# Attention inside a four-layer kernel: the value products of a step are joined and moved behind the far bias of the step's second piece

## The chip, the cores and the metric

The kernel runs on one core of a Trainium2 chip. The metric is the device time of one execution in microseconds (us). TensorE is called PE in the profile, VectorE is DVE, ScalarE is ACT, GpSimd is POOL, and SyncE (SP) issues the DMAs.

## The reference

Four layers run one after the other; the change touches only the first, an attention with a relative position bias, for 2 batches of 2048 tokens, 16 heads of 16 columns:

```
qkv = x @ W_w.T + W_b                                  # q, k, v: 16 heads of 16
attn = einsum('bhqd,bhkd->bhqk', q, k) / sqrt(256)     # causal: keys after the query are -inf
attn = attn + rpb[key - query + s - 1]                 # one bias per head and distance, clamped at the table's end
w = softmax(attn, axis=-1)
o = einsum('bhqk,bhkd->bhqd', w, v)                    # then projection, residual, layer norms
```

The other three layers (a mixture of cumulative products, a state-space scan, a mixture of 20 experts) follow it and are not changed.

## The kernel before

Each head `p` of the attention takes 10 steps of 4 slots (`STEPS`, `SLOTS`), and each slot works on both batches (`b` is 0 or 1). Two jobs share the slots. For head `p` the *scores* are made with keys on the partitions: a piece is a pair (J, c) of a tile of 128 keys and a chunk of 512 queries, of which only the causal part, 128 to 512 columns, is computed. `SCORED` says which piece stands in which slot. For head `p + 1` the *search* makes the same products with queries on the partitions, so that DVE can find each query's maximum in time for the next head; `SEARCHED` is its order. Its widths in slots 0 to 3 match those that `SCORED` has in the same slots.

On PE one slot is: `score` for b = 0 (L541) beside `search` for b = 1 (L515), then `score` for b = 1 beside `search` for b = 0. The two of a pair use different halves of the array's rows and run side by side; below this is "a pair". Then comes `add_near` (L527), the bias of the searched piece, four matmuls, where that piece has one, and then `add_far` (L557), the bias of the scored piece, twelve matmuls on quarters of the array, where the piece has queries at least 8 tiles after the keys. Only pieces (0, 2), (0, 3), (1, 2), (1, 3), (2, 2), (2, 3), (3, 2), (3, 3), (4, 3), (5, 3), (6, 3) and (7, 3) have such a far bias: two in each of steps 2 to 5, one in each of steps 6 to 9, none in steps 0 and 1.

The *sums* (L584) multiply the probabilities of the step before by the values. A step has two rounds of them. A round is four products, which go to four different groups of 32 columns of the array and run side by side; each product of f32 data is two matmul instructions (a half each). `sums(p, step - 1, turn)` for turn 0 stands between the two pairs of slot 1, and for turn 1 between the two pairs of slot 3.

The results lie in PSUM in two rings of three banks (`RING = 3`). ACT takes the exponential of each score (`exponential`, L644) into `prob`, which is why `score` waits for the exponential of three scores earlier. DVE reduces each searched piece to its row maximum (`largest`, L733; L736 with the causal mask where the piece lies on the diagonal), which is why `search` waits for the reduction of three searches earlier. Turns of the maxima (`turn_max`, L593) and of the outputs (`turn_out`, L600) take their turn in the search's ring. Every engine works strictly in the order of its loop; a wait on PE holds back everything that stands behind it on PE. POOL clears the part above the diagonal (`cut`, L432). `prob` has two buffers, one for each of two neighbouring steps. SP issues the loads of the next heads; the change moves none of them.

Of the kernel before, what the change touches and what calls it, by code (L numbers as in the profile page):

```python
# [66 lines left out]
def after(eng, sem, value):  # L67

    if not isinstance(value, int) or value > 0:
        eng.wait_ge(sem, value)  # L70
# [35 lines left out]
def phase_qkv(nc, t):  # L106
# [14 lines left out]
PAIRS = H  # L121
# [6 lines left out]


SCORED = [[(8, 2), (9, 2), (8, 3), (9, 3)], [(11, 2), (10, 2), (10, 3), (11, 3)],  # L130
# [4 lines left out]
assert [sorted(pieces) for pieces in SCORED] == [[(J, c) for J in keys for c in range(J // TPC, S // CH)] for keys in GROUPS_OF_KEYS]  # L135
SEARCHED = [(15, 0), (14, 3), (15, 1), (15, 2),
# [10 lines left out]
STEPS, SLOTS = len(SCORED), 4  # L147
# [57 lines left out]
def phase_attention(nc, t):  # L205
# [3 lines left out]
    with nc.cleanup_on_exit(), ExitStack() as ctx:  # L209
# [55 lines left out]
        def half(b, rows=P // 2):  # L265
            return slice(b * P // 2, b * P // 2 + rows)
# [203 lines left out]
        def _(eng):  # L470
# [61 lines left out]
            def score(p, step, x, b):  # L532

                J, c = SCORED[step][x]
                lo, hi = max(J * P, c * CH), (c + 1) * CH
                has_far = (J + FAR) * P < hi
                turn = NP2 * p + 2 * (SLOTS * step + x) + b
                after(eng, s2_read, turn - RING + 1)
                if turn == 0:
                    eng.wait_ge(s1_read, ALONE)  # L540
                mm = nc.tensor.matmul(s2[:, turn % RING, 0:hi - lo], ks[p % 3][half(b, ROWS), J * P:(J + 1) * P],  # L541
                                      qs[p % 3][half(b, ROWS), lo:hi], start=True, stop=not has_far)
                if not has_far:
                    mm.then_inc(s2_ready, 1)

            def add_far(p, step, x):

                J, c = SCORED[step][x]
                lo, hi = max(J * P, c * CH), (c + 1) * CH
                far_lo = max(lo, (J + FAR) * P)  # L550
                turn = NP2 * p + 2 * (SLOTS * step + x)
                for part in range(3 if far_lo < hi else 0):
                    for b in range(2):
                        for s in range(2):
                            at = far_lo - (J + FAR) * P + s * P // 2
                            rows = half(1 - s)
                            mm = nc.tensor.matmul(s2[rows, (turn + b) % RING, far_lo - lo:hi - lo], flip_b[half(b), s, rows],  # L557
                                                  far[p % 2][half(b), part, at:at + hi - far_lo], start=False, stop=part == 2)
                        if part == 2:
                            mm.then_inc(s2_ready, 1)  # L560

            def sums(p, step, turn):

                if turn == 0:
                    eng.wait_ge(s2_read, NP2 * p + 2 * SLOTS * (step + 1))
                    eng.wait_ge(cut_done, CUTS[STEPS] * p + CUTS[step + 1])
                if step == 0 and turn == 0:
                    eng.wait_ge(vst_ready, 2 * p + 2)
                    for b in range(2):
                        after(eng, oT_ready[b], p)  # L570
                keys = GROUPS_OF_KEYS[step]
                for b in range(2):
                    for x, (J, c) in enumerate(SCORED[step]):
                        if len(keys) == 1:
                            first = b == 0
                        elif keys[1] - keys[0] == 1:
                            first = J == keys[0]
                        else:
                            first = (J == keys[0]) == (b == 0)
                        if first != (turn == 0):  # L580
                            continue
                        g = c if b == 0 else 3 - c
                        lo = max(J * P - c * CH, 0)
                        mm = nc.tensor.matmul(o_ps[32 * g:32 * g + 32, b, lo:CH], vst[p % 2][b][:, J, :],  # L584
                                              prob[:, b, step % 2, x * CH + lo:(x + 1) * CH],
                                              start=J == (8 if c >= 2 else 0), stop=J == (3, 7, 7, 15 if b == 0 else 7)[c])
                mm.then_inc(summed, 1)
# [15 lines left out]
            for p in range(-1, PAIRS + 1):  # L603
                if p + 1 < PAIRS:
                    eng.wait_ge(stack_ready, 2 * p + 4)
                    eng.wait_ge(near_loaded[(p + 1) % 2], 32 * ((p + 1) // 2 + 1))
                for step in range(STEPS):
                    if 0 <= p < PAIRS and step in (0, 2):
                        eng.wait_ge(row_ready, 4 * p + 2 + step)
                        eng.wait_ge(far_loaded[p % 2], 96 * (p // 2 + 1))  # L610
                    for x in range(SLOTS):
                        for b in range(2):
                            if 0 <= p < PAIRS:
                                score(p, step, x, b)
                            if p + 1 < PAIRS:
                                search(p + 1, SLOTS * step + x, 1 - b)
                            if b == 0 and x in (1, 3) and p >= 0:
                                if step > 0 and p < PAIRS:
                                    sums(p, step - 1, x // 2)
                                if step == 0 and p > 0:  # L620
                                    sums(p - 1, STEPS - 1, x // 2)
                        if p + 1 < PAIRS:
                            add_near(p + 1, SLOTS * step + x)
                        if p == -1 and x % 2 == 1:
                            project(len(USES) - 20 + (SLOTS * step + x) // 2)
                        if 0 <= p < PAIRS:
                            add_far(p, step, x)
                        if (step, x) == (0, 2) and 0 <= p < PAIRS:
                            turn_max(p, 0)
                        if (step, x) == (7, 2) and p + 1 < PAIRS:  # L630
                            turn_max(p + 1, 1)
                        if step == 1 and x in (1, 3) and p > 0:
                            turn_out(p - 1, x // 2)
# [2131 lines left out]
```

## Time and profile before

| | us |
|---|---|
| median of 3 runs | 2643.36 (2638.0 to 2645.14) |
| the profiled execution: span from first to last instruction | 2646.7 (no other time of it is listed) |
| attention, its 16 heads of scores | about 121 to 1085 of the span |
| one head | 60.5 |
| PE busy, whole span | 2472.2 (93%) |
| DVE busy, whole span | 1964.7 (74%) |
| ACT busy, whole span | 1382.1 (52%) |

PE's busy time counts each matmul from its start until its result has landed, so that overlapping matmuls and the tail of the last one are in it; the distance from one start to the next is the better measure of what a piece of PE work costs. A row of the timeline with a count merges neighbouring instructions of one kind; its time runs from the start of the first to the end of the last.

### The profile page before, as it was taken

The page shows a single profiled execution, that of the slowest core. Times are in us where ns is not written, and L with a number is a line of the kernel's source. Part 1 is how long each engine was busy: PE and PEld are TensorE (multiplying, and loading weights), DVE is VectorE, ACT ScalarE, POOL GpSimd, SP SyncE. Part 2 cuts the span into 40 slices and gives each one's busy share as a digit, 9 for nine tenths or more (in the row PEclk, how much of TensorE's full clock was granted, in tenths as well). Part 3 has the DMA queues.
Part 4 walks back from the last instruction along what each step waited for, and adds up shares of the span by engine and source line. Part 5 has one row for each costly group of instructions (what it writes and reads, how often), then busy time and mean ns, then how long its engine had stood idle before and what let it go on. Part 6 is the DMA issues. An engine that isn't in the chain of part 4 may idle for free. (4 is left out here: it accounts for less than half of the span.)

```text
span 2646.7 us, 43896 instructions
## 1 busy us (share of the span) xinstructions
PE 2472.2 (93%) x15059; PEld 1552.6 (59%) x15059; DVE 1964.7 (74%) x4037; ACT 1382.1 (52%) x2469; POOL 1110.7 (42%) x1092
## 2 busy tenths in 40 slices
PE   7999999999999999899999997999999999977992
PEld 4433333333333333467777775888888888855772
DVE  3777777777777774266676657999999999975256
ACT  3466666666666666444455535655555555543320
POOL 3522222222222221110000004999989898944454
PEclk9999999999999999999999998999999999987996
DMA  8633333323333321100000000000000000024785
GB/s 244 174 70 71 82 58 58 58 58 58 58 58 69 70 64 66 54 16 17 16 24 25 9 17 8 13 12 12 12 12 12 12 12 12 4 86 130 238 282 162
DMA packets 109601, 166.41 MB, mean 63 GB/s; under 512 B 15876, under 2 KB 74296, under 8 KB 106232
## 3 DMA queue, kind: packets, MB, share of 16 engines
q1 hardware_dynamic: 99064, 143.24, 21.5%
q0 software_dynamic: 6144, 16.79, 2.0%
q10 hardware_dynamic: 4224, 4.19, 0.5%
q8 instruction: 99, 1.62, 0.3%
q14 instruction: 70, 0.57, 0.1%
HBM read 97.66 MB, written 62.01 MB: 60 GB/s over the span
## 5 line engine op out<-in xcount | busy, mean ns | idle before, releaser
L644 ACT ACTIVATE ssm_in_dt<-att_s 128x512 f32<-128x512 f32 (+3 forms) x1280 | 610.0, 535 | 346.9 <-PE att_s L541 182.7
L733 DVE TENSOR_REDUCE att_partmax<-att_s 128x1 f32<-128x512 f32 x768 | 494.3, 686 | 109.8 <-PE att_s L515 66.4
L541 PE MATMUL att_s<-att_qs,att_ks 49*128 49x512 f32 (+3 forms) x1280 | 433.9, 419 | 16.1 <-ACT ssm_in_dt L644 13.8
L515 PE MATMUL att_s<-att_ks,att_qs 49*128 49x512 f32 (+3 forms) x1280 | 434.5, 424 | 4.9 <-DVE att_qs L723 4.7
L541 PEld LDWEIGHTS att_s<-att_qs,att_ks 49*128 49x128 f32 x1280 | 207.4, 185 | 380.3 <-ACT ssm_in_dt L644 307.6
L1797 POOL TENSOR_TENSOR ssm_cc<-ssm_cc,ssm_h 128x512 f32<-128x512 f32 x256 | 334.9, 1308 | 75.7 <-DVE ssm_h L1858 73.8
L432 POOL TENSOR_SCALAR_AFFINE_SELECT ssm_in_dt<-ssm_in_dt 128x256 f32<-128x256 f32 x256 | 104.6, 409 | 621.5 <-ACT ssm_in_dt L644 562.8
L584 PE MATMUL att_o_ps<-ssm_in_dt,att_vst 128*32 128x512 f32 (+3 forms) x2560 | 340.6, 542 | 5.3 <-ACT ssm_in_dt L644 5.3
L1812 POOL TENSOR_TENSOR ssm_out_z<-ssm_out_z,ssm_cc 128x512 f32<-128x512 f32 x256 | 340.4, 1330 | 0.1
L1737 ACT ACTIVATE ssm_cc<-ssm_c_ps,ssm_cur 128x512 f32<-128x512 f32 x256 | 199.0, 777 | 211.8 <-PE ssm_c_ps L1686 211.5
L736 DVE CUSTOM_DVE_ANT_0 att_hid<-att_s,att_hidden 128x512 bf16<-128x512 f32 (+3 forms) x512 | 238.8, 487 | 94.6 <-PE att_s L515 93.7
L1858 DVE TENSOR_TENSOR_SCAN ssm_h<-ssm_a_ps,ssm_h,ssm_inp 128x512 f32<-128x512 f32 x192 | 243.8, 1270 | 0.1
L1730 ACT ACTIVATE ssm_a_ps<-ssm_in_dt,ssm_cur 128x512 f32<-128x512 f32 x256 | 176.4, 689 | 114.5 <-DVE ssm_h L1858 108.5
L515 PEld LDWEIGHTS att_s<-att_ks,att_qs 49*128 49x128 f32 x1280 | 203.9, 185 | 28.1 <-DVE att_partmax L733 10.8
L1842 DVE SCALAR_TENSOR_TENSOR ssm_inp<-ssm_b_ps,ssm_cur,ssm_in_u 128x512 f32<-128x512 f32 x256 | 190.0, 742 | 34.5 <-PE ssm_b_ps L1686 32.7
L1684 PE MATMUL ssm_b_ps<-ssm_hi,ssm_w_hi 128*128 128x512 f32 x512 | 203.5, 398 | 12.7 <-DVE ssm_lo L1835 11.2
L1684 PE MATMUL ssm_c_ps<-ssm_hi,ssm_w_hi 128*128 128x512 f32 x512 | 203.2, 397 | 0.0
L1685 PE MATMUL ssm_c_ps<-ssm_lo,ssm_w_hi 128*128 128x512 f32 x512 | 203.2, 397 | 0.0
L1686 PE MATMUL ssm_c_ps<-ssm_hi,ssm_w_lo 128*128 128x512 f32 x512 | 202.9, 396 | 0.0
L1686 PE MATMUL ssm_b_ps<-ssm_hi,ssm_w_lo 128*128 128x512 f32 x512 | 202.8, 396 | 0.0
L1685 PE MATMUL ssm_b_ps<-ssm_lo,ssm_w_hi 128*128 128x512 f32 x512 | 202.4, 395 | 0.0
L1850 DVE SCALAR_TENSOR_TENSOR ssm_inp<-ssm_a_ps,ssm_inp 128x512 f32<-128x512 f32 x256 | 169.2, 661 | 0.0
(324 smaller groups left out, 4183.7 us busy)
## 6 DMA issues: line engine op xcount, KB each, us to landing
qk_halves<-ssm_in_dt SPq DMA_DIRECT2D x64, 256.0 KB
moe_sorted<-att_hidden SPq DMA_DIRECT2D x31, 512.0 KB, 9.4
moe_rows<-moe_sorted SPq DMA_DIRECT2D x62, 256.0 KB
moe_answers<-moe_mixed SPq DMA_DIRECT2D x62, 256.0 KB
att_far<-bias_tables SPq DMA_DIRECT2D x96, 136.0 KB, 8.5
att_stage_q<-qk_halves SPq DMA_DIRECT2D x96, 128.0 KB, 4.4
att_stage_k<-qk_halves SPq DMA_DIRECT2D x96, 128.0 KB, 5.9
ssm_raw<-in_w_bc SPq DMA_DIRECT2D x30, 256.0 KB, 2.6
```

What stands on the lines that cost most here:

```text
L515: mm = nc.tensor.matmul(s1[:, S1_BANK[at], 0:hi - lo], qs[p % 3][half(b, ROWS), I * P:(I + 1) * P], ks[p % 3][half(b, ROWS), lo:hi], start ...
L541: mm = nc.tensor.matmul(s2[:, turn % RING, 0:hi - lo], ks[p % 3][half(b, ROWS), J * P:(J + 1) * P], qs[p % 3][half(b, ROWS), lo:hi], start ...
L584: mm = nc.tensor.matmul(o_ps[32 * g:32 * g + 32, b, lo:CH], vst[p % 2][b][:, J, :], prob[:, b, step % 2, x * CH + lo:(x + 1) * CH], start= ...
L644: nc.scalar.activation(prob[:, b, step % 2, x * CH + lo:(x + 1) * CH], s2[:, turn % RING, 0:CH - lo], ACT.Exp, scale=1.0 / HD).then_inc(s2 ...
L733: nc.vector.tensor_reduce(most, piece, AX, ALU.max).then_inc(s1_read, 1)
L736: nc.vector.tensor_tensor_reduce(out=hid[HID[at]][:, 0:width], in0=piece, in1=hidden[:, CH - width:CH], scale=1.0, scalar=-3.0e38, op0=ALU ...
L1684: nc.tensor.matmul(out, w_hi, hi[:, k, tok], start=first, stop=False)
L1685: nc.tensor.matmul(out, w_hi, lo[:, k, tok], start=False, stop=False)
L1686: return nc.tensor.matmul(out, w_lo, hi[:, k, tok], start=False, stop=last)
L1797: nc.gpsimd.tensor_tensor(at, at, h[:, i % H_RING], ALU.mult).then_inc(multiplied, 1)
L1812: nc.gpsimd.tensor_tensor(part, part, cc[:, i % Y_RING], ALU.add).then_inc(y_added, 1)
L1858: nc.vector.tensor_tensor_scan(h[:, i % H_RING], a_ps[:, i % A_RING], inp[:, i % 2], 0.0 if first else h[:, (i - 1) % H_RING, CH - 1:CH], ...
```

## The change

The far pieces of steps 2 to 9 change places with their neighbours, so that slot 1 always holds one of them. Both rounds of sums now stand together, once per step, behind the far bias of slot 1 (in steps 0 and 1, which have no far bias, behind slot 1's pairs and near bias). `SEARCHED` stays as it was.

```diff
 SCORED = [[(8, 2), (9, 2), (8, 3), (9, 3)], [(11, 2), (10, 2), (10, 3), (11, 3)],
-          [(0, 2), (0, 0), (0, 3), (0, 1)], [(1, 2), (1, 0), (1, 3), (1, 1)],
-          [(2, 2), (2, 0), (2, 3), (2, 1)], [(3, 2), (3, 0), (3, 3), (3, 1)],
-          [(4, 3), (4, 1), (12, 3), (4, 2)], [(5, 3), (5, 1), (13, 3), (5, 2)],
-          [(6, 3), (6, 1), (14, 3), (6, 2)], [(7, 3), (7, 1), (15, 3), (7, 2)]]
+          [(0, 0), (0, 2), (0, 3), (0, 1)], [(1, 0), (1, 2), (1, 3), (1, 1)],
+          [(2, 0), (2, 2), (2, 3), (2, 1)], [(3, 0), (3, 2), (3, 3), (3, 1)],
+          [(4, 1), (4, 3), (12, 3), (4, 2)], [(5, 1), (5, 3), (13, 3), (5, 2)],
+          [(6, 1), (6, 3), (14, 3), (6, 2)], [(7, 1), (7, 3), (15, 3), (7, 2)]]
...
                                 score(p, step, x, b)
                             if p + 1 < PAIRS:
                                 search(p + 1, SLOTS * step + x, 1 - b)
-                            if b == 0 and x in (1, 3) and p >= 0:
-                                if step > 0 and p < PAIRS:
-                                    sums(p, step - 1, x // 2)
-                                if step == 0 and p > 0:
-                                    sums(p - 1, STEPS - 1, x // 2)
                         if p + 1 < PAIRS:
                             add_near(p + 1, SLOTS * step + x)
                         if p == -1 and x % 2 == 1:
                             project(len(USES) - 20 + (SLOTS * step + x) // 2)
                         if 0 <= p < PAIRS:
                             add_far(p, step, x)
+                        if x == 1 and p >= 0:
+                            for turn in range(2):
+                                if step > 0 and p < PAIRS:
+                                    sums(p, step - 1, turn)
+                                if step == 0 and p > 0:
+                                    sums(p - 1, STEPS - 1, turn)
```

## Rows read from the trace of the kernel before

**Rows 1.** Stretches: heads 1 to 14, and the last head; busy us by engine.

```profile
core 0: us, PE busy (x) PEld busy (x) DVE busy (x) ACT busy (x) POOL busy (x), PEclk, DMA share, GB/s
182.00:1030.00 848.00, 825.75 (x7310) 330.44 (x7310) 667.41 (x1736) 538.94 (x1134) 209.76 (x334) 1.00 0.32 61
1030.00:1076.00 46.00, 43.83 (x346) 15.04 (x344) 3.45 (x12) 33.47 (x69) 6.97 (x14) 1.00 0.26 95
```

**Rows 2.** Groups by line in 182 to 1030: busy us, mean ns, idle before.

```profile
L515 PE MATMUL att_s<-att_ks,att_qs 49*128 49x512 f32 (+3 forms) x1121 | 387.8, 419 | 0.0
L541 PE MATMUL att_s<-att_qs,att_ks 49*128 49x512 f32 (+3 forms) x1121 | 382.0, 416 | 11.8 <-ACT ssm_in_dt L644 9.9
L584 PE MATMUL att_o_ps<-ssm_in_dt,att_vst 128*32 128x512 f32 (+3 forms) x2240 | 298.0, 540 | 4.3 <-ACT ssm_in_dt L644 4.3
...
L733 DVE TENSOR_REDUCE att_partmax<-att_s 128x1 f32<-128x512 f32 x672 | 433.2, 686 | 89.8 <-PE att_s L515 60.7 <-PE att_s L527 27.1
...
L644 ACT ACTIVATE ssm_in_dt<-att_s 128x512 f32<-128x512 f32 (+3 forms) x1120 | 533.9, 535 | 309.1 <-PE att_s L541 162.0 <-PE att_s L557 146.6
```

**Rows 3.** Timeline of one step: start us, length us, engine, line, count.

```profile
520.85 0.84 PE L557 MATMUL att_s<-att_far,att_flip_b 64*64 64x512 bf16 x12
521.62 0.50 PE L541 MATMUL att_s<-att_qs,att_ks 49*128 49x512 f32 x1
521.73 1.57 ACT L644 ACTIVATE ssm_in_dt<-att_s 128x512 f32<-128x512 f32 x3 [1.35 <-PE att_s L557]
522.05 1.06 PE L584 MATMUL att_o_ps<-ssm_in_dt,att_vst 128*32 128x512 f32 x8
523.05 0.49 PE L541 MATMUL att_s<-att_qs,att_ks 49*128 49x512 f32 x1
523.39 0.61 PE L541 MATMUL att_s<-att_qs,att_ks 49*128 49x512 f32 x2
523.58 0.60 ACT L644 ACTIVATE ssm_in_dt<-att_s 128x512 f32<-128x512 f32 x1 [0.28 <-PE att_s L541]
523.61 0.69 DVE L733 TENSOR_REDUCE att_partmax<-att_s 128x1 f32<-128x512 f32 x1 [0.73 <-PE att_s L515]
523.62 0.39 PE L515 MATMUL att_s<-att_ks,att_qs 49*128 49x512 f32 x1
523.84 0.62 PE L527 MATMUL att_s<-att_near,att_flip_b 64*128 64x512 bf16 x4
```

**Rows 4.** The same timeline, a window later.

```profile
524.07 0.39 PE L527 MATMUL att_s<-att_near,att_flip_b 64*128 64x512 bf16 x2
524.39 0.84 PE L557 MATMUL att_s<-att_far,att_flip_b 64*64 64x512 bf16 x12
524.48 1.29 DVE L733 TENSOR_REDUCE att_partmax<-att_s 128x1 f32<-128x512 f32 x2 [0.17 <-PE att_s L527]
525.16 0.50 PE L541 MATMUL att_s<-att_qs,att_ks 49*128 49x512 f32 x1
...
525.33 0.60 ACT L644 ACTIVATE ssm_in_dt<-att_s 128x512 f32<-128x512 f32 x1 [1.15 <-PE att_s L557]
525.59 0.64 PE L584 MATMUL att_o_ps<-ssm_in_dt,att_vst 128*32 128x512 f32 x4
```

**Rows 5.** Timeline where a search waits for DVE, and a turn of outputs (L600).

```profile
549.13 1.29 DVE L733 TENSOR_REDUCE att_partmax<-att_s 128x1 f32<-128x512 f32 x2 [0.32 <-PE att_s L527]
...
549.88 0.18 PEld L515 LDWEIGHTS att_s<-att_ks,att_qs 49*128 49x128 f32 x1 [0.29 <-DVE att_partmax L733]
...
554.61 0.66 PE L600 MATMUL att_s<-att_ident,att_oT 128*128 128x128 f32 x4
...
555.20 0.49 PE L541 MATMUL att_s<-att_qs,att_ks 49*128 49x512 f32 x1
```

**Rows 6.** The turn of the maxima (L593), same place in two neighbouring heads.

```profile
533.50 0.27 PE L593 MATMUL att_s<-att_ident,att_mx 128*16 128x128 f32 x1 [0.43 <-DVE att_partmax L736]
...
594.05 0.27 PE L593 MATMUL att_s<-att_ident,att_mx 128*16 128x128 f32 x1 [0.43 <-DVE att_partmax L736]
```

**Rows 7.** Timeline after the last score: two rounds of sums back to back.

```profile
1084.06 1.28 PE L584 MATMUL att_o_ps<-ssm_in_dt,att_vst 128*32 128x512 f32 x16 [0.69 <-ACT ssm_in_dt L644]
```

## The prediction

> **What bounds the kernel now.** I read first the busy time of the stretch that the change touches. In heads 1 to 14 PE is busy 825.75 of 848 us, DVE 667.41 and ACT 538.94, with PE's clock at 1.00, the 2.4 GHz level [rows 1]. The groups by line come next: PE's idle time before its matmuls is 11.8 us before L541, 4.3 before L584 and 0.0 before L515 [rows 2], while DVE waited 89.8 us before its reductions and ACT 309.1 us before its exponentials, both for PE. So PE sets the pace, and it hardly waits. One head takes 594.05 - 533.50 = 60.55 us [rows 6], about 16 times.
>
> The third view is the timeline, for starts [rows 3]. A pair that follows work of another shape (far bias or sums) is followed by its neighbour 0.34 us later (523.05 to 523.39); the next pair of the same shape comes 0.23 us after that (523.39 to 523.62). A far bias of 512 columns takes 0.77 (520.85 to 521.62). From the pair at 521.62 to the sums is 0.43, and one round of sums holds PE for 1.00 (522.05 to 523.05). So each change of shape costs about 0.1 us on either side of the sums.
>
> The reader should also see what the sums do for the others. While PE is in a round, DVE and ACT empty their rings of three banks: from 521.73 ACT does three exponentials in 1.57 us, one every (1.57 - 0.60) / 2 = 0.48 us [rows 3], and DVE does two reductions in 1.29 us, one every 0.61 us [rows 4]. Eight searches of 512 columns are 4.9 us of DVE in a step of some 6 us, and two rounds, one in each half of the step, give it that time without PE waiting. That is why PE shows no wait although only three banks stand between.
>
> **What the change removes on PE.** Before, each round costs its 1.00 plus 0.10 to enter and 0.10 in the next pair: 2.40 us for two. Behind a far bias the joined rounds cost only their own length over what "far bias, pair" costs already. That length: the first half of a round lasts 0.64 and the whole 1.06, so a further half adds 0.42 to 0.43 [rows 3, 4]; joined is 1.00 + 2 x 0.43 = 1.86. Saved: 0.54 us in steps 2 to 9. In steps 0 and 1, with no far bias, 0.33. Where widths differ more is saved: 16 matmuls of the last step (products of 512 and 128 columns, each group of columns having one of either) took 1.28 against 1.06 for 8 [rows 7], so the groups run on by themselves, and the joined rounds of the steps with 384, 256 and 128 take some 1.65, 1.43 and 1.24: 0.2 + 0.4 + 0.6 = 1.2 us per head.
>
> On the other side, scores of 512 columns now run beside searches of 384, 256 or 128 in slot 1, and the reverse in slot 0 (steps 3 to 5 and 7 to 9). A pair lasts as long as its wider part; with the halves alternating this costs the difference once, some 0.05, 0.11 and 0.16 us, twice each: 0.6 us. On PE alone the sum per head is 8 x 0.54 + 2 x 0.33 + 1.2 - 0.6 = 5.6 us less, if PE then waits no more than now. The number of far biases, near biases, exponentials, reductions, cuts and DMAs is the same. The cuts come as early or earlier, and the sums ask for them later; `prob` is freed in time (the sums of step s - 2 stand before step s); the copies of the outputs become ready sooner. These are worth nothing, as POOL and SP are idle for most of this stretch (POOL 209.76 of 848 us [rows 1]).
>
> **What it adds: waits in the two rings.** Now PE is away for 1.86 us once, in which DVE can do at most the three searches in its banks, and from there to the next sums come six pairs in a row (slots 2, 3, 0) and two more in slot 1 with nothing between but biases. I work out the time from one joined block to the next, from sums of step 2 to those in step 3, with zero at the start of the block. Used are: pairs 0.34 and 0.23 apart; near bias 0.23 to its second set; that set to DVE 0.41 (524.07 to 524.48 [rows 4]); last far set to ACT 0.42 (its merged row of 0.84 less one matmul of 0.38 puts the last set 0.46 in; 520.85 + 0.46 to 521.73 [rows 3]); reduction 0.69, one per 0.61; from its end to the waiting search 0.06 (549.13 + 0.69 to 549.88 [rows 5]), together 0.74 from a reduction's start.
> - 0 to 1.86: sums. DVE and ACT end by 0.5 and 1.2, then stand idle.
> - Slot 2: pairs at 1.86 and 2.19, near bias 2.42 and 2.65, so DVE starts the first reduction at 3.06 and the second at 3.67. Far bias 2.95 to 3.73; ACT's first exponential at 3.83, the second at 4.31.
> - Slot 3: pair at 3.73; the second pair must wait for that first exponential (3.83 + 0.65 = 4.48). Its reductions start at 4.3 and 5.05.
> - Slot 0: pairs at 4.96 and 5.44, each held by an exponential. The near bias follows, last set at 5.73; DVE starts at 6.14.
> - Slot 1: the second search takes the bank of slot 0's first search, so it waits until 6.14 + 0.74 = 6.88. Then 0.17 of its own, 0.09 to change shape and 0.61 of far bias (384 columns): the next sums start at 7.76.
>
> The trace of before has 6.63 between these places. The same reckoning done for the old order, from the sums of slot 3 in step 2 to those in step 3, gives 6.46; the trace has 6.51, so the method is good to about 1%.
>
> The other steps, worked the same way: DVE's restart, the start of slot 0's first reduction, plus 0.74 (0.35 where it is 128 wide), plus pair and far bias; new time against old:
> - step 3 to 4: 3.06, 6.20, tail 0.66: 7.60 against 6.43
> - 4 to 5 (no near bias in slot 2): 2.42, 5.76, 0.44: 6.94 against 5.72
> - 5 to 6: 2.98, 6.20, 1.09: 8.03 against 6.67
> - 6 to 7: 3.01, then four reductions 5.44, 0.87: 7.05 against 5.75
> - 7 to 8: 2.42, 4.82, 0.66: 6.22 against 5.75
> - 8 to 9: 2.19, 4.12, 0.44: 5.30 against 4.86
> - 9 to 0: 1.99, 4.03, 0.28: 5.05 against 4.71
> - 0 to 1: 2.45, 5.68 (a copy of DVE in between), 0.21: 6.24 against 6.24
> - 1 to 2: the two turns of outputs, 0.59 each (554.61 to 555.20 [rows 5]), delay both ends: 3.65, 6.99, 1.09: 8.82 against 7.80
>
> The differences are 1.13 + 1.17 + 1.22 + 1.36 + 1.30 + 0.47 + 0.44 + 0.34 + 0.00 + 1.02 = 8.45 us per head, 69.0 against 60.6. The 5.6 us saved on PE are in it: the new waits are some 14 us per head. Heads 0 to 14 have a search: 15 x 8.45 = 127 us. In the last head DVE has nothing to reduce (3.45 us busy [rows 1]) and only ACT's ring holds; the same walk gives +0.8 to +1.3 in four steps, a little less than nothing in three, together +4. Sum +131 us: span 2646.7 to 2777, and from the median of the runs, which is 3 us lower, 2643.4 + 131 = 2774.
>
> The unknown prices are the joined length, which lies between 1.43 (the second round costs only its two later halves at half price) and 2.00 (twice the single round), and the reckoning's own 1%, which is 0.7 us a head. As DVE is idle through the block's end, 0.1 us more or less in it is 1 us a head and 15 us in all: -0.3 gives 2730, +0.14 and the loss of the 1.2 us for unequal widths gives 2815. I take 1.86, from the nearest rows [rows 3, 4].
>
> The Trainium skill speaks on both sides. TensorEngine Tiling (Array Packing), section Key Properties, says that a change of the tiling mode drains the engine; the 0.1 us on each side of the sums agree, and by that rule alone the change gains. The same page, PSUM Bottleneck, says that tiling speeds up TensorE but not the emptying of PSUM, which can become the limit; by that rule it loses. The sum above stands on the rows without either.
>
> **Rivals.**
> 1. *Fewer changes of shape are all that counts* (faster). If the rings never held PE: 5.6 x 16 = 90 us less, 2554. For it: PE busy 97% and hardly a wait [rows 1, 2]. Against: that state exists because the sums are spread; eight pairs at 0.23 to 0.34 apart outrun a DVE that needs 0.61 for each.
> 2. *Only ACT's ring holds* (about even). If DVE caught up better than I reckon, exponentials at 0.48 would set the pace: steps 2 to 5 still lose 0.5 to 0.7 each, since slot 2's far bias delays the first exponential to 3.83; the other six gain 3 us together. That is -0.6 us a head, 2634. Against: DVE's reductions are longer than the exponentials, and the wait behind the near bias of slot 0 is one of DVE.
> 3. *The joined rounds don't overlap at all* (slower still): 2815, as above. Against: rows 7.
>
> That the change doesn't do what it says is excluded by the order of the loop.
>
> **How the numbers follow.** Forecast 0.83; rival 3 0.05; rival 2 0.07, about half of it within the bound; rival 1 0.05. A measurement of this kernel tells 0.3%, 8 us, from no change. Slower 0.88, same 0.04, faster 0.08. The likeliest case alone gives 2735 to 2815; the range is 2705 to 2822, on account of a DVE that I have made a little too slow, or two banks that come free sooner.
>
> **What would show it.** The turn of the maxima (L593) should come 69 us after that of the head before. The sums should appear as 16 in one row of about 1.9 us. PE's idle time before L515 should go from 0.0 to several us per head, released by DVE, L541's by ACT; DVE should be idle for 1 to 2 us around each block of sums. PE busy in attention should fall below 90%. I am wrong if the head is near 61 us or less: then the banks were not the limit. I am wrong in the size if the search of slot 1 doesn't wait for the reduction of slot 0.

## The result, and the profile after

The change makes the kernel slower: 2909.16 us, the median of 4 runs (2904.08 to 2913.04), against 2644.01 us for the kernel before in 4 runs (2638.0 to 2645.14). The ratio is 1.0997 (95% interval 1.0974 to 1.102). That is 265 us where I had forecast 131. The sign was right, and so was the mechanism that was forecast, waits at the two rings; but it accounts for half of the loss. The other half comes from something that the forecast did not contain.

The head of the page of the changed kernel, and three stretches of it: heads 1 to 14 without the end, 50 us inside head 0, and most of the last head. Columns as in rows 1; the last but two is PE's granted clock.

```profile
span 2911.3 us, 43896 instructions
...
PE 2706.7 (93%) x15059; PEld 1674.4 (58%) x15059; DVE 1950.5 (67%) x4037; ACT 1364.2 (47%) x2469; POOL 1109.3 (38%) x1092
...
PEclk9999889989889899877999999899999999997997
```

```profile
core 0: us, PE busy (x) PEld busy (x) DVE busy (x) ACT busy (x) POOL busy (x), PEclk, DMA share, GB/s
182.00:1000.00 818.00, 778.41 (x5509) 330.79 (x5505) 494.43 (x1316) 395.08 (x857) 164.38 (x257) 0.89 0.27 52
132.00:182.00 50.00, 47.63 (x385) 19.90 (x389) 32.72 (x75) 26.23 (x54) 9.20 (x16) 1.00 0.33 64
1275.00:1350.00 75.00, 71.30 (x394) 26.88 (x392) 3.60 (x14) 36.93 (x82) 8.50 (x18) 0.70 0.16 58
```

In the 818 us from 182 to 1000 PE issued 5509 matmuls; before it issued 7310 in 848 [rows 1]. It still counts as busy for 95% of the time, because a matmul at the lower clock lasts longer and is counted for longer. The granted clock is 0.89 where it was 1.00, and 0.70 in the last head.

The groups by line in 182 to 1000 (busy us, mean ns, idle before), to set beside rows 2; ACT's line moved from L644 to L645, DVE's from L733 to L734:

```profile
L645 ACT ACTIVATE ssm_in_dt<-att_s 128x512 f32<-128x512 f32 (+3 forms) x846 | 391.3, 541 | 424.3 <-PE att_s L557 269.4 <-PE att_s L541 153.6
L515 PE MATMUL att_s<-att_ks,att_qs 49*128 49x512 f32 (+3 forms) x846 | 354.8, 458 | 25.2 <-DVE att_partmax L734 18.7 <-DVE att_partmax L737 2.7
L734 DVE TENSOR_REDUCE att_partmax<-att_s 128x1 f32<-128x512 f32 x506 | 322.7, 684 | 198.9 <-PE att_s L527 167.7 <-PE att_s L515 29.0
L541 PE MATMUL att_s<-att_qs,att_ks 49*128 49x512 f32 (+3 forms) x846 | 320.1, 429 | 12.3 <-ACT ssm_in_dt L645 11.0
L584 PE MATMUL att_o_ps<-ssm_in_dt,att_vst 128*32 128x512 f32 (+3 forms) x1696 | 248.9, 680 | 0.0
```

Three things differ. L515 was never late and now has 25.2 us of idle time before it, most of it ended by DVE. DVE, whose reductions last as long as before (684 and 686 ns), is idle for 198.9 us before 506 of them, where it was idle for 89.8 us before 672. And a matmul of the sums lasts 680 ns on average instead of 540. Neither waiting nor the joining explains that: between 132 and 182 us, with the clock at 1.00, the joined ones last 550:

```profile
L584 PE MATMUL att_o_ps<-ssm_in_dt,att_vst 128*32 128x512 f32 (+3 forms) x100 | 12.2, 550 | 0.0
```

A head, from one turn of the maxima (L593) to the next at the same place [rows 6], now takes 330.58 - 252.73 = 77.85 us, before 60.55:

```profile
252.73 0.28 PE L593 MATMUL att_s<-att_ident,att_mx 128*16 128x128 f32 x1
...
330.58 0.28 PE L593 MATMUL att_s<-att_ident,att_mx 128*16 128x128 f32 x1
```

**The same block in two lengths.** First the joined sums of steps 2 to 9 of head 0 and of the next head's step 0, on PE's timeline (start us, length us). The rows between are left out:

```profile
137.62 1.93 PE L584 MATMUL att_o_ps<-ssm_in_dt,att_vst 128*32 128x256 f32 x16
...
145.43 1.92 PE L584 MATMUL att_o_ps<-ssm_in_dt,att_vst 128*32 128x512 f32 x16
...
153.09 1.92 PE L584 MATMUL att_o_ps<-ssm_in_dt,att_vst 128*32 128x384 f32 x16
...
160.08 1.92 PE L584 MATMUL att_o_ps<-ssm_in_dt,att_vst 128*32 128x256 f32 x16
...
168.36 1.93 PE L584 MATMUL att_o_ps<-ssm_in_dt,att_vst 128*32 128x128 f32 x16
...
175.69 1.92 PE L584 MATMUL att_o_ps<-ssm_in_dt,att_vst 128*32 128x512 f32 x16
...
181.95 1.71 PE L584 MATMUL att_o_ps<-ssm_in_dt,att_vst 128*32 128x384 f32 x16
...
187.22 1.50 PE L584 MATMUL att_o_ps<-ssm_in_dt,att_vst 128*32 128x256 f32 x16
...
192.35 1.28 PE L584 MATMUL att_o_ps<-ssm_in_dt,att_vst 128*32 128x128 f32 x16
```

The distances from start to start are 7.81, 7.66, 6.98, 8.28, 7.33, 6.25, 5.27 and 5.13 us. The forecast had 7.76, 7.60, 6.94, 8.03, 7.05, 6.22, 5.30 and 5.05. Here the clock is 1.00. Of the other two distances, step 0 to 1 is 6.27 to 6.28 wherever the clock stays at 1.00 (forecast 6.24); step 1 to 2 (forecast 8.82) has some time at the lower level in every head, and is 9.5 or more in heads 1 to 14.

Then steps 4 and 5 of head 2:

```profile
302.25 3.59 PE L584 MATMUL att_o_ps<-ssm_in_dt,att_vst 128*32 128x384 f32 x16
...
306.44 0.84 PE L557 MATMUL att_s<-att_far,att_flip_b 64*64 64x512 bf16 x12
307.21 0.50 PE L541 MATMUL att_s<-att_qs,att_ks 49*128 49x512 f32 x1
...
307.96 0.50 PE L541 MATMUL att_s<-att_qs,att_ks 49*128 49x512 f32 x1 [0.25 <-ACT ssm_in_dt L645]
...
308.45 0.32 PE L541 MATMUL att_s<-att_qs,att_ks 49*128 49x128 f32 x1
...
308.94 0.32 PE L541 MATMUL att_s<-att_qs,att_ks 49*128 49x128 f32 x1
...
309.12 0.56 PE L527 MATMUL att_s<-att_near,att_flip_b 64*128 64x256 bf16 x4
...
309.61 1.29 DVE L734 TENSOR_REDUCE att_partmax<-att_s 128x1 f32<-128x512 f32 x2 [0.38 <-PE att_s L527]
...
310.36 0.33 PE L515 MATMUL att_s<-att_ks,att_qs 49*128 49x128 f32 x1 [0.25 <-DVE att_partmax L734]
310.61 0.36 PE L557 MATMUL att_s<-att_far,att_flip_b 64*64 64x128 bf16 x12
```

And PE's clock in the block itself, in the pairs behind it, and in the step's end:

```profile
302.25:305.78 3.53, 3.53 (x21) 0.92 (x18) 0.47 (x4) 1.08 (x2) 0.00 (x0) 0.52 0.00 0
305.78:307.90 2.12, 1.93 (x20) 0.74 (x18) 1.41 (x3) 0.58 (x2) 0.00 (x0) 1.00 0.00 0
307.90:310.90 3.00, 2.68 (x26) 1.50 (x26) 2.57 (x7) 1.82 (x6) 0.41 (x1) 1.00 0.01 3
```

The block at 302.25 does the same as the one at 153.09 (both stand in step 4) and lasts 3.59 instead of 1.92 us, at a granted clock of 0.52: nearly all of it lies at the lower of PE's two levels, 1.2 instead of 2.4 GHz. Behind it the clock is 1.00 again, and in slot 3 and the next slot 0 come pairs 0.49 to 0.75 us apart, where pairs of one shape follow each other after 0.23 when nothing holds them [rows 3]. The second pair of slot 3 (307.96) waits for the exponential behind slot 2's far bias, as reckoned (0.75 after the first; the forecast had 4.48 - 3.73). The search at 310.36 waits for the reduction of slot 0 that began at 309.61: 0.75 later, the forecast had 0.74.

**The split.** A block holds PE from its start to the start of the next matmul (154.95 behind the block at 153.09: 1.86), 0.07 us less than its row shows. By that measure 85 of the 160 joined blocks last 1.21, 1.43, 1.64 or 1.85 us, by step, and 75 last longer, up to 3.6; the mean is 2.30. Before, 317 of 318 rounds lasted 0.99 to 1.00. For each of the ten steps I take the fastest time from its first score to that of the next step in heads 1 to 14 (for step 7, mostly slow, 7.08) and get a head of 69.5 us at the upper level, against 60.5 before and 69.0 forecast. So in heads 0 to 14 the rings cost some 9.0 x 15 = 135 us, net of what the joining saves, and with the forecast's 4 us for the last head 139. The clock's part is what is left: heads 1 to 14 took 237 us more, 9.0 x 14 = 126 of it the rings, so 111; and the last head took 74.6 us against 52.8, where +4 was forecast, so 18. Together 129 us.

The trace bears this out more directly. Heads 1 to 14 and the last head of the changed kernel:

```profile
189.72:1274.83 1085.11, 1032.63 (x7310) 438.70 (x7309) 655.32 (x1737) 523.60 (x1135) 209.27 (x335) 0.89 0.25 48
1274.83:1349.41 74.58, 70.88 (x394) 26.59 (x391) 3.77 (x14) 36.60 (x81) 8.20 (x18) 0.71 0.16 58
```

Heads 1 to 14 issue the same 7310 matmuls as before in 1085.11 instead of 848. The clock stands at its lower level for 239 us of them and for 44 us of the last head, before for none of either; at half speed that can cost at most half, 119 and 22 us. And the excess lies where the clock fell: 74 of the 140 steps have no time at the lower level, and they are 0.04 us longer on average than the fastest of their kind, 3 us in all; the 66 others are 109 us longer in all.

Beside the rows on the clock: the Trainium skill, TensorE: Matmul & The Clock Gate, A second HAM failure mode: psum-queue depth-cycling, tells of a kernel that cycles through PSUM banks and in which PE idles for so short and so often between groups of matmuls that its clock swings between two levels. The blocks above, 1.92 us at 1.00 and 3.59 us at 0.52, agree with it. I had read the rings of PSUM banks as waits and not as a danger to the clock.

### The profile page after: what moved, and what is told of

Its sections match the earlier page's. It is cut to its first block and busy times, and to the rows that moved or that the text cites. A ratio compares the mean times of both kernels' runs of the same rounds, so it can differ in the third digit from the quotient of the medians.

```text
span 2911.3 us, 43896 instructions
## 1 busy us (share of the span) xinstructions
PE 2706.7 (93%) x15059; PEld 1674.4 (58%) x15059; DVE 1950.5 (67%) x4037; ACT 1364.2 (47%) x2469; POOL 1109.3 (38%) x1092
## 5 line engine op out<-in xcount | busy, mean ns | idle before, releaser
L645 ACT ACTIVATE ssm_in_dt<-att_s 128x512 f32<-128x512 f32 (+3 forms) x1280 | 592.3, 541 | 632.1 <-PE att_s L557 402.6
L734 DVE TENSOR_REDUCE att_partmax<-att_s 128x1 f32<-128x512 f32 x768 | 489.5, 684 | 298.2 <-PE att_s L527 249.5
L515 PE MATMUL att_s<-att_ks,att_qs 49*128 49x512 f32 (+3 forms) x1280 | 521.7, 460 | 37.8 <-DVE att_partmax L734 26.2
L541 PE MATMUL att_s<-att_qs,att_ks 49*128 49x512 f32 (+3 forms) x1280 | 489.7, 440 | 22.5 <-ACT ssm_in_dt L645 20.0
L541 PEld LDWEIGHTS att_s<-att_qs,att_ks 49*128 49x128 f32 x1280 | 227.9, 192 | 287.6 <-ACT ssm_in_dt L645 165.0
L584 PE MATMUL att_o_ps<-ssm_in_dt,att_vst 128*32 128x512 f32 (+3 forms) x2560 | 379.1, 685 | 0.7 <-ACT ssm_in_dt L645 0.7
L515 PEld LDWEIGHTS att_s<-att_ks,att_qs 49*128 49x128 f32 x1280 | 220.3, 190 | 162.1 <-DVE att_partmax L734 119.6
L737 DVE CUSTOM_DVE_ANT_0 att_hid<-att_s,att_hidden 128x512 bf16<-128x512 f32 (+3 forms) x512 | 228.6, 484 | 122.7 <-PE att_s L515 121.2
L584 PEld LDWEIGHTS att_o_ps<-ssm_in_dt,att_vst 128*32 128x32 f32 x2560 | 100.9, 128 | 171.3 <-issue 152.5
```

Of the source, the lines that this page charges most:

```text
L515: mm = nc.tensor.matmul(s1[:, S1_BANK[at], 0:hi - lo], qs[p % 3][half(b, ROWS), I * P:(I + 1) * P], ks[p % 3][half(b, ROWS), lo:hi], start ...
L645: nc.scalar.activation(prob[:, b, step % 2, x * CH + lo:(x + 1) * CH], s2[:, turn % RING, 0:CH - lo], ACT.Exp, scale=1.0 / HD).then_inc(s2 ...
L734: nc.vector.tensor_reduce(most, piece, AX, ALU.max).then_inc(s1_read, 1)
L737: nc.vector.tensor_tensor_reduce(out=hid[HID[at]][:, 0:width], in0=piece, in1=hidden[:, CH - width:CH], scale=1.0, scalar=-3.0e38, op0=ALU ...
```

## Experiments

Each run is compared with the kernel before on the same chip. "Head" is the mean over heads 1 to 13, 60.56 us in the kernel before.

**1. The order of the pieces alone.** The change's `SCORED`; the single rounds stay between the pairs of slots 1 and 3.

```diff
-          [(0, 2), (0, 0), (0, 3), (0, 1)], ...
+          [(0, 0), (0, 2), (0, 3), (0, 1)], ...
```

> The new order of pieces (far bias in slot 1), the sums in their old places (one round between the pairs of slot 1, one between those of slot 3). Theory A (the loss comes from joining the rounds: PE waits at the two rings, and the waits let TensorE's clock fall): the order alone costs only unequal widths in a pair, 0.6 us a head, so 2644 + 10 = 2654, heads of 61 to 62 us, rounds of sums all at 1.00 us. Theory B (the loss comes from the order of the pieces, a far bias ahead of slot 2's searches): at least half of the 265 us is here, 2770 or more.

Measured: 2756.63 against 2632.02, ratio 1.0469 (1.0451 to 1.0486); head 68.23. The expectation missed by 100 us: I had taken the order as nearly free. The rows show the wait, at full clock (groups by line, then timeline):

```profile
182.00:1000.00 818.00, 763.15 (x6264) 300.44 (x6264) 576.77 (x1488) 451.33 (x971) 181.94 (x287) 1.00 0.30 56
```

```profile
L541 PE MATMUL att_s<-att_qs,att_ks 49*128 49x512 f32 x960 | 383.0, 434 | 49.9 <-ACT ssm_in_dt L644 44.6
```

```profile
575.30 0.84 PE L557 MATMUL att_s<-att_far,att_flip_b 64*64 64x512 bf16 x12
576.07 0.50 PE L541 MATMUL att_s<-att_qs,att_ks 49*128 49x512 f32 x1
...
576.83 0.50 PE L541 MATMUL att_s<-att_qs,att_ks 49*128 49x512 f32 x1 [0.25 <-ACT ssm_in_dt L644]
```

After a far bias in slot 1 two pairs follow with no sums between them. In the old order the round in slot 1 stood right behind the first pair after slot 0's far bias and filled ACT's time. In heads 1 to 14 every block is at full speed and no time is spent at the lower level, so these 7.7 us a head are no matter of the clock: they are waits, and the unequal widths in a pair, for which the forecast had 0.6.

**2. The joining alone.** Old `SCORED`, the changed kernel's place for the sums.

```diff
-                            if b == 0 and x in (1, 3) and p >= 0:
-                                ... sums(p, step - 1, x // 2)
...
+                        if x == 1 and p >= 0:
+                            for turn in range(2):
+                                ... sums(p, step - 1, turn)
```

> The old order of pieces, both rounds of sums joined at the end of slot 1. Theory A: nearly all of the loss is here; the search of slot 1 still waits for slot 0's reduction, and the second score for an exponential behind slot 0's far bias, so 2880 +- 40, and the blocks of sums come in two lengths, about 1.86 and up to 3.5 us. Theory B: near 2644.

Measured: 2852.81, ratio 1.0846 (1.0809 to 1.0882); head 74.86, clock 0.92 in 182 to 1000. A hit. The fastest steps add up to 69.5 us a head. So at full clock the order alone costs 7.7 a head, the joining alone 9.0, and both together 9.0: their prices don't add, as if each removed the same cover. The falls of the clock come with the joining: 1.00 in experiment 1, 0.92 here. Waits alone don't bring them, since experiment 1 has nearly as many.

**3. DVE's work cut down, in the changed kernel.** Each reduction reads 128 columns (part of the row maximum is left out). The joined blocks and PE's work stay as they are.

```diff
-                width = min(CH, (I + 1) * P - g * CH)
+                width = P
```

> The changed kernel, but DVE reduces only the first 128 columns of each searched piece (part of the maximum is left out), so that a bank of the search comes free some 0.4 us sooner and DVE's work falls from 0.61 to about 0.21 us a piece. Theory A: DVE's ring no longer holds PE, only ACT's does (rival 2 of the prediction: heads of about 60 us at full clock), and the clock falls seldom: 2640 to 2700. Theory C (the waits are those of ACT's ring, or the joined block is simply dearer than thought): hardly any change, 2850 to 2909.

Measured: 2682.16, ratio 1.0186 (1.0169 to 1.0203); head 63.29, clock 0.99. A hit: with PE's work unchanged the kernel is 50 us above the one before and not 265. Part of that DVE's shorter work would gain in any kernel (experiment 11, where ACT's work is cut as well, gives an upper bound, 38 us). DVE's ring is the main holder, and with its waits gone the clock nearly stays up as well: 24 us of heads 1 to 14 at the lower level instead of 239, with the joined blocks still there. The last head, in which DVE has nothing to reduce, keeps its loss. It takes 73.5 us against 52.8 before, 21 of the 50 us:

```profile
1066.23:1139.74 73.51, 69.19 (x394) 25.20 (x392) 2.98 (x14) 36.39 (x81) 8.41 (x18) 0.75 0.17 59
```

**4. More work for PE in the gaps.** Four more pairs of scores of slot 1's piece, into the banks of slot 1's scores, behind them and before their far bias, in steps 2 to 9 of heads 0 to 14.

```diff
+                            if 0 <= p < PAIRS - 1 and step >= 2 and (x, b) == (1, 1):
+                                for n in range(AGAIN):
+                                    again(p, step, x, n < AGAIN - 1)
...
```

> The changed kernel; in steps 2 to 9 of heads 0 to 14 the two scores of slot 1 are computed five times each (four times too many, same banks, same values), ahead of the search that waits longest. That is 0.9 us of PE work in what was PE's idle time, so that at full clock it costs nothing or up to 0.3 us a step. Theory A (about half of the loss, 134 us, is TensorE's clock at its lower level after these waits): the blocks of sums keep 1.86 us, heads fall from 77 to about 70, 2780 to 2830. Theory D (the clock is not the missing half; the waits are longer at full clock too): no gain, 2909 or up to 40 us more.

Measured: 2862.16, ratio 1.0876 (1.0858 to 1.0894). The kernel with more work is 1.1% faster than the one without. The expected 2780 to 2830 was missed, but so was the rival's "no gain". In heads 0 to 14 steps 2 to 9 have no slow block left; the four pairs overfill the gaps, which makes a step some 0.4 us longer, and step 1, which got none, is still slow in 12 of 14 heads.

**5. Two extra pairs instead of four** (the edit is against experiment 4).

```diff
-AGAIN = 4
+AGAIN = 2
```

> As the run with four extra pairs of scores, but only two: 0.46 us of work in slot 1's wait of 0.59 us (the four took 0.93 us and held the search back by up to 0.35 us a step). Theory A (all that is missing from the prediction is the clock): steps 2 to 9 keep full-speed blocks of sums of 1.86 us and lose the 0.3 us a step, heads near 72 (69.3 of the ring reckoning, plus step 1, which has no extra work and stays slow), 2815 to 2840. Theory D (the four filled no clock, they only moved waits): the same as with four, 2862, or back to 2909.

Measured: 2852.79 against 2645.48, ratio 1.0767 (1.0731 to 1.0804); above the 2815 to 2840 that I expected. The total doesn't decide between the two theories; the blocks do. Its stretch, and the groups of its sums (L593) and extra scores (L552):

```profile
182.00:1000.00 818.00, 785.76 (x6148) 362.15 (x6148) 519.47 (x1378) 414.31 (x899) 169.36 (x268) 0.95 0.27 52
```

```profile
L593 PE MATMUL att_o_ps<-ssm_in_dt,att_vst 128*32 128x512 f32 (+3 forms) x1776 | 228.8, 604 | 0.0
...
L552 PE MATMUL att_s<-att_qs,att_ks 49*128 49x512 f32 x359 | 90.4, 412 | 0.0
```

A matmul of the sums lasts 604 ns instead of 680. In steps 2 to 6 all 70 blocks are at full speed, with distances of 7.85, 7.65, 6.98, 8.29 and, where the clock stays up to step 7, 7.34 us: those of the changed kernel at full clock, with the waits now partly filled. The blocks of steps 1, 7 and 9 are still slow in 14, 9 and 8 of 14 heads.

**6. Joined, but between the pairs of slot 1.** The new order of the pieces, and the block where the single round had stood.

```diff
+                            if b == 0 and x == 1 and p >= 0:
+                                for turn in range(2):
+                                    if step > 0 and p < PAIRS:
+                                        sums(p, step - 1, turn)
```

> The new order of pieces, both rounds joined, but between the pairs of slot 1 instead of behind its far bias. Ring theory: the second search of slot 1 no longer waits (1.86 us of sums cover slot 0's reduction), but the far bias of slot 1 comes after the block, its exponentials then hold slot 2's second pair (0.42 us, as in the run with the new order alone), and one more change of shape is paid: full-clock heads of about 69 to 70, with the idle time spread in smaller pieces, so the clock falls less often than in the changed kernel: 2800 to 2880. If joining as such is what counts and not the place: 2909.

Measured: 2935.19, ratio 1.1099 (1.1076 to 1.1122); head 78.35. A miss, above 2880 and above the rival's 2909: this is slower than the change, so the place behind the far bias is not by itself what hurts. PE has the lowest clock of all runs, and in each of heads 2 to 14 the blocks of steps 0, 1, 7 and 9 are slow (2.29, 3.21, 2.97 and 2.72 us) and those of 2 to 6 and 8 at full speed:

```profile
182.00:1000.00 818.00, 767.00 (x5433) 327.77 (x5431) 502.80 (x1303) 386.80 (x847) 162.20 (x256) 0.87 0.27 50
```

**7. The same changes of shape saved, rounds kept apart.** Old order, single rounds behind the far bias of slot 0 and at the end of slot 2, in steps 2 to 9.

```diff
                             add_far(p, step, x)
+                            if step >= 2 and x in (0, 2):
+                                sums(p, step - 1, x // 2)
...
```

> The old order of pieces; in steps 2 to 9 each single round of sums directly behind the far bias of slot 0 and at the end of slot 2, not joined. Ring theory: the changes of shape saved are worth 0.2 us a round, but four pairs now follow each other with no far bias among them, and the fourth waits some 0.4 to 0.5 us for the reduction and the exponential of the second: about 0.5 us a step lost, 2660 to 2740. If the changes of shape are all that counts: 2590.

Measured: 2712.86, ratio 1.0256 (1.0239 to 1.0274); head 64.77, clock 1.00. A hit. Apart, the rounds keep the clock up, but moved by half a slot they already cost 4.2 us a head net. The wait is one for ACT:

```profile
L541 PE MATMUL att_s<-att_qs,att_ks 49*128 49x128 f32 (+2 forms) x1010 | 347.7, 420 | 41.9 <-ACT ssm_in_dt L646 40.5
```

**8. Far bias late instead of sums early.** In the kernel before, the far bias of slots 0 and 2 is moved behind the next slot's first pair, straight before the round.

> The kernel before, with the far bias of slots 0 and 2 moved behind the first pair of the next slot, directly ahead of the sums: pair, far bias, sums, pair in place of far bias, pair, sums, pair. One change of shape less per far bias (12 a head), 0.1 to 0.2 us each, and every round of sums stays between two pairs, so that no ring waits: 1.2 to 2.4 us a head, 20 to 40 us faster than before, 2595 to 2615. If the rings do bind (a score is ready 0.3 us later): no gain, 2632.

```diff
+                            if b == 0 and x in (1, 3) and 0 <= p < PAIRS:
+                                add_far(p, step, x - 1)
...
-                        if 0 <= p < PAIRS:
-                            add_far(p, step, x)
```

Measured: 2690.18, ratio 1.0166 (1.0149 to 1.0183); head 63.32. A miss: 75 us above the upper end of what was expected. The idle time shown hardly grew (12.1 us before the scores, now L546), but a score lasts 440 ns on average where it lasted 416, and a search 445 where it lasted 419 [rows 2]. The extra time lies in steps 2 to 9, those with a moved far bias: 0.1 to 0.6 us in each, 2.8 together, and none in steps 0 and 1. I take it that the later exponentials hold the next scores; no run separated which ring holds which pair.

**9. Extra scores in every step.** As experiment 4, with two extra pairs in steps 2 to 6 and three in steps 7 to 9; in steps 0 and 1 the last score of slot 1 is made two and three times more.

```diff
+AGAIN = (2, 3, 2, 2, 2, 2, 2, 3, 3, 3)
...
```

> The changed kernel with extra scores in all steps of heads 0 to 14 (two pairs in slot 1, three in steps 7 to 9; in steps 0 and 1 the last score of slot 1 two and three times more than needed, before its result is released). Theory A (the missing half is the clock): steps 1, 7, 8 and 9, which stayed slow in the run with two extra pairs, now keep full-speed sums too; heads of 70 to 71.5 us, 2780 to 2815 with the last head still slow. If the slow blocks have another cause: 2850 or more, heads of 74.

Measured: 2850.95, ratio 1.0787 (1.0769 to 1.0805). A miss, and at 2850 the value that I had set down for slow blocks with another cause than the missing work. The blocks of step 1 are still slow in 4 of 14 heads, of step 2 in 5, of step 7 in 9, at a lower granted clock as before; why the filling doesn't reach them stays open.

**10 and 11. What is the saving worth without rings?** Reductions and exponentials of 128 columns (the rest of each is left out), in the changed kernel and in the kernel before.

```diff
-                nc.scalar.activation(prob[..., x * CH + lo:(x + 1) * CH], s2[:, turn % RING, 0:CH - lo],
+                nc.scalar.activation(prob[..., x * CH + lo:x * CH + lo + (CH - lo if p == 0 else P)], s2[:, turn % RING, 0:CH - lo if p == 0 else P],
...
-                width = min(CH, (I + 1) * P - g * CH)
+                width = P
```

> The changed kernel, with 128 columns a piece for DVE's reductions and for ACT's exponentials (in heads 1 to 15 the other probabilities are left as they were; part of the computation is left out). Both rings then let PE go early. Ring theory: the waits nearly vanish and what is left is the saving on PE that the prediction reckoned, 5.6 us a head against the kernel before: heads of 55 to 57, 2555 to 2600. If the joined rounds cost PE more than was reckoned, the head stays at 60 or more.

> The kernel before with the same narrow reductions and exponentials. It hardly waited at the rings: of the 60.5 us a head some 3 to 5 are waits in steps 0, 1 and 7 to 9; heads of 56 to 58, 2560 to 2600. The difference to the changed kernel with the same edit is the price of the changes of shape by itself: 1 to 3 us a head in the changed kernel's favour if its near-bias waits are not gone entirely, up to 5.6 if they are.

Measured: 2607.23, ratio 0.9862 (0.9846 to 0.9879), and 2606.49, ratio 0.9855 (0.9839 to 0.9872). Both lie some 7 us above what was expected. Heads of 57.94 and 58.36 us; by the fastest steps 57.3 and 58.3. So of the saving 0.4 to 1.0 us a head show, and not 5.6. I take it that waits behind the near bias, which these kernels keep, stand in the way of the rest; no run shows it. The whole kernels are equal.

**12. Still more filling.** As 9, with four extra pairs in step 7, four extra scores in step 1, and single repeated scores in other slots of steps 0, 1 and 6 to 9.

```diff
+AGAIN = (2, 4, 2, 2, 2, 2, 2, 4, 3, 3)
+ONE = {(0, 3, 0): 1, (0, 3, 1): 1, (1, 0, 0): 1, (1, 0, 1): 2, (1, 1, 0): 1, ...}
...
```

> As the run before with extra scores, and more of them in the stretches that stayed slow: four pairs in slot 1 of steps 1 and 7, and single repeated scores (0.23 us each) in steps 0, 1 and 6 to 9, where a search waits for DVE and the score beside it does not. Theory A (the clock is what is missing): sums of steps 1 and 7 at full speed too, heads of 70.5 to 71.5 us instead of 73.1, 2815 to 2830 (the last head has no extra work and stays slow). If the slow blocks of steps 1 and 7 come from something else: 2851 or more.

The group of its sums, 561 ns a matmul where the changed kernel has 680:

```profile
L598 PE MATMUL att_o_ps<-ssm_in_dt,att_vst 128*32 128x512 f32 (+3 forms) x1808 | 214.3, 561 | 0.0
```

Measured: 2854.99, ratio 1.0778 (1.0752 to 1.0803). A miss in time, again at the value set down for another cause (2851 or more), but it shows whole heads. Heads 1 and 12 have no slow block in any of their ten steps; head 1 takes 71.57 us, its filling included. In the 12 others of heads 1 to 14 the slow blocks are 8 of step 1, 3 of step 8 and 2 others. What keeps the mean at 73.14 is mostly step 1: 9.6 to 11.2 us in those 8 heads, 8.0 in the rest.

## Why the prediction was half right

- *PE sets the pace and has no wait because the sums are spread.* Borne out. Moving a single round by half a slot (experiment 7) costs 67 us, and what precedes it (experiment 8) 45.
- *The reckoning of the rings.* Right to 0.1 us in seven of nine distances at full clock; 0.25 and 0.28 low in 5 to 6 and 6 to 7. The tenth, 1 to 2, at 8.82 against 9.5 or more, stood nowhere wholly at full clock. Waits came where they were put: the second pair of slot 3 for ACT, slot 1's second search for slot 0's reduction. Heads of 69.5 against 69.0. For the last head's +4 no run gives the ring's part by itself.
- *The joined block, 1.86 us.* Right where the clock is up: 1.85. Unequal widths do overlap: 1.64, 1.43 and 1.21 against the 1.65, 1.43 and 1.24 forecast. Rival 3 falls.
- *Rival 1 and rival 2.* Rival 2 falls with experiment 3, where relieving DVE alone takes most of the loss away. Rival 1's 5.6 us a head were not found even with short reductions and exponentials: 0.4 to 1.0.
- *The order of the pieces* had no term of its own; alone it costs 125 us. The sum for the rings came out right because it was walked for the new order; that the order alone would cost nearly as much was not seen.
- *"PE busy in attention should fall below 90%."* Wrong: 95%. I had used the busy share, which lengthens with the clock's fall, as if it were work. The count of matmuls in the stretch shows the loss.
- *The last head, +4.* Wrong: +21.8, at a clock of 0.70.

**The step that failed** is in the first paragraph of the prediction: "with PE's clock at 1.00, the 2.4 GHz level". It is true of the kernel before, and every duration of the reckoning was then used as if the changed kernel would have it too. Nowhere did I ask whether 14 us more of short waits per head leave the clock where it is. They don't: in heads 1 to 14 the blocks of steps 1, 3, 4, 7 and 9 are slow in 9, 10, 9, 13 and 8 of 14 heads, those of the other steps in fewer, and only step 0 has none. A term of 0 stood where 129 us belonged. The runs bear that term out from two sides: with the gaps filled (experiment 5) steps 2 to 6 keep their ring distances and lose only the slow blocks; and the four kernels with more work in them (4, 5, 9, 12) have ratios of 1.077 to 1.088 where the changed kernel has 1.0997. The 129 us themselves are a difference, which the time at the lower level allows (at most 119 and 22 us); no run brought all heads to full clock with nothing else changed.

Nor is it the waits alone. Experiment 1 has 7.7 us a head of loss and experiment 7 has 4.2, with rounds of 1.00 us, and no time of heads 1 to 14 at the lower level; experiment 3 has the joined blocks without DVE's long waits, and 24 us instead of 239. The falls came where both were there.

**Open:** why step 1 is slow when every step has been filled. It has the two turns of outputs and the longest distance (9.5 us or more), and head 0, which has no such turns, keeps 1.00 from about 132 us to step 2 of the next head. No run took the turns away. Open too is why the fall comes in one step and not in another. PE's work just before gives no hint of it. The stretch of 3.9 us before the slow block at 302.25, and the same stretch of head 0, before the fast one at 153.09:

```profile
298.34:302.25 3.91, 3.50 (x32) 1.77 (x28) 3.46 (x7) 2.62 (x6) 0.41 (x1) 1.00 0.00 0
149.17:153.09 3.92, 3.51 (x32) 1.77 (x28) 3.47 (x7) 2.62 (x6) 0.41 (x1) 1.00 0.00 0
```

They hold the same matmuls and the same idle time, within 0.01 us; the clock fell behind the first alone. What differs is further back: the block of step 3 had been slow in head 2 (2.79 us at 293.75) and not in head 0 (145.43). Whether that matters was not tested. No version that computes everything beats the kernel before.

## What to carry to other kernels

Where one engine shows no wait although small rings couple it to slower ones, look for the work of another kind that is spread between: it is what hides the others, and joining it to save changes of shape can take the cover away. Before costing a change that puts short waits on PE, price it at both levels of PE's clock: this kernel ran at 1.00 with its work spread, and with short waits alone, but not with the waits between long blocks. And judge PE by matmuls per us, not by its busy share.

## What the runs showed of the hardware

- The clock fell while PE counted as busy for 95% of the time and the waits in the steps shown are 0.25 us each. In the 3.9 us before the fall at 302.25 PE was busy for 3.50; in a stretch with the same work, 3.51 of 3.92 us busy, no fall followed.
- Waits of this size left the clock at 1.00 where the sums stood in single rounds (experiments 1 and 7, heads 1 to 14).
- Extra matmuls whose results nobody reads made the kernel faster: a ratio of 1.0767 (1.0731 to 1.0804) with two pairs a step, 1.0997 (1.0974 to 1.102) with none.
- Two rounds of sums of unequal widths, on four groups of 32 columns, run on without waiting for each other's wider parts: 16 matmuls in 1.28 us (192.35) where 8 had taken 1.06 [rows 3].
